# A new order for the front of a convolution and quantised matmul kernel, with the conv in two parts

## The chip, the core and the metric

The kernel runs on one core of a Trainium2 chip. The metric is the time of one execution on the device, in microseconds (us).

Five engines work side by side, each through its own list of instructions in order: TensorE (PE, with its weight loads as PEld), VectorE (DVE), ScalarE (ACT), GpSimd (POOL) and SyncE (SP), which here only issues transfers. An instruction can wait for a semaphore that another engine raises; everything behind it on its own engine then waits too.

## The reference, cut to what matters

```python
# x: (64, 64, 1024)   conv in 4 groups of 16 channels, 9 taps, pad 4
out = conv(x, weight) + (cond @ c_weight.T)[:, :, None] + cond_bias[None, :, None]
def fake_quant(v, bits, axis):          # integer levels times a scale
    bound = 2 ** (bits - 1) - 1
    scale = max(abs(v), axis) / bound
    return round(clip(v / scale, -bound, bound)) * scale
xq = fake_quant(out, 8, axis=-1)        # one scale per row of 1024
kq = fake_quant(kernel, 8, axis=0)      # (1024, 1024), one scale per output column
y = xq @ kq + fake_quant(bias, 16, axis=-1)
result = x + fake_quant(y, 8, axis=-1)
```

## The kernel before

The 4096 rows of 1024 are cut into 32 tiles of 128 rows (`TILES`): 8 samples times the 16 channels of one conv group. In all loops `t` is a tile and `k` a step; the work of one tile is spread over six or more steps.

For one tile, in the order in which the data flows:

- `load_xwin(t)` (SP, L170) brings the windows of x. `round_x(t)` (ACT, L287) makes the rounded part `x_hi`; `split(t)` (POOL, L229) makes the rest `x_lo` from both.
- `conv(t)` (PE, L404) is 2 matmuls for the condition term (`select` against `ctx2`), then three groups of 4: `x_hi` with `w_hi`, `x_hi` with `w_lo`, `x_lo` with `w_hi`. Only the last group needs `x_lo`. The result takes 2 of the PSUM banks `conv_ps`, which two tiles use in turn.
- `column_max(t)` (DVE, L602) takes the largest magnitudes, `spread_max(t)` (PE, L429) brings them across partitions, `levels(t)` (DVE, L619) makes the inverse scale and the integer levels of samples 0 to 3, and `round_levels(t)` (ACT, L325) those of samples 4 to 7.
- `turn_levels(t)` (PE, L437) transposes the levels into `turn_ps`, `take_levels(t)` (ACT, L317) copies them to `a_t`.
- `dense(t, h)` (PE, L447) is 8 matmuls for half `h` of the 1024 output columns. `scale_half(t, h)` (DVE, L583) applies the scales; `add_bias` adds the quantised bias, on DVE for half 0 and on POOL for half 1.
- `out_scale(t)` (DVE, L649), `quantise(t)` (ACT, L335: two activations of 1024) and `add_x(t)` (POOL, L245) finish the tile, and SP stores it. `outs(k)` says which tiles do so in step `k`. It is one tile in a step, except in steps 15 and 20, where it is two, since the second halves of `dense` catch up by one step at tiles 10 and 16 (`CATCH_UP`).

Beside this stands the front, done once. The 1024 x 1024 matrix is loaded as 8 blocks in 4 pairs, 1 MB each (`load_k`). `k_levels(pair)` (DVE, L555) waits for a pair, takes its maxima, makes scale and inverse, and rounds those of its two blocks that are in `DVE_K`; `k_round(fb)` (ACT, L294) rounds the others (`ACT_K`). `k_turn(user)` (PE, L461) transposes a block into a PSUM bank of `dense_ps` and `k_take(user)` (ACT, L299) copies it to `kq`; two of the ten users are the scales themselves. Since `dense_ps` is also where `dense` writes, the users from 5 on have one bank, and each waits for the take of the one ahead. `bias_scale` (DVE) and `bias_levels` (ACT) quantise the bias, which a transfer of 512 KB spreads over all partitions. The condition term is two small matmuls on PE, then three DVE instructions (L542 to L547) that end in `ctx_made`, for which `conv(0)` waits. `warm_up` (L389) is 2 matmuls of ident by ident, twice.

The whole order of work is written out by hand in one list per engine (DVE from L683, ACT from L352, PE from L492, POOL from L252, SP from L174). The front lies in steps 0 to 4: `k_levels(k + 1)` stands behind `column_max(k)` on DVE, and the users of the bank lie between the convs and the dense halves on PE.

Of the kernel before, what the change touches and what calls it, by code (L numbers as in the profile page):

```python
# [32 lines left out]
ACT_K = (1, 3)  # L33
DVE_K = (0, 2, 4, 5, 6, 7)
# [4 lines left out]
def build(nc, xw, xr, wt, cond_t, cw_t, cond_bias, ker, bias, out):  # L39
    with ExitStack() as ctx:  # L40
# [6 lines left out]
        def sem(name):  # L47
# [27 lines left out]
        b_row = sb("b_row", [P, F], F32)  # L75
# [27 lines left out]
        turn_ps = ps("turn_ps", [P, NS, P], I16)  # L103

# [5 lines left out]
            "k_turned", "k_taken", "b_max_made", "b_scale_made", "b_inv_made",  # L110
# [44 lines left out]
        def k_bank(user):  # L155
            return dense_ps[:, user % 2 if user < 5 else 1, :]

        K_USERS = (0, 1, 2, 3, "scale0", 4, 5, 6, 7, "scale1")
# [5 lines left out]
        def _(sp):  # L164
# [51 lines left out]
        def _(pool):  # L216
# [50 lines left out]
        def _(act):  # L267
            act.dma_start(condt[:], cond_t).then_inc(s["cond_in"], 16)
# [40 lines left out]
            def bias_levels():  # L309
                act.wait_ge(s["b_inv_made"], 1)  # L310
                act.activation(b_int[:], b_row[:], ACT.Copy, scale=b_stat[:, 2:3]
# [45 lines left out]
            for k in range(second_step(LAST) + 2):  # L357
                if k == 2:
                    take_levels(1)
                    k_take(5)  # L360
                    k_take(6)
                    round_x(4)
                    bias_levels()
                elif k == 3:
                    k_take(7)
                    k_take(8)
                    take_levels(2)
                    round_x(5)
                else:
                    if k == 4:  # L370
                        k_take(9)
                    if there(k - 1):
                        take_levels(k - 1)
                    if there(k + 2):
                        round_x(k + 2)
                if k == 0:
                    k_round(3)
                    k_take(2)
                    k_take(3)
                    k_take(4)  # L380
                for t in outs(k):
                    quantise(t)
                if there(k):
                    round_levels(k)
            quantise_last()

        @block.tensor
        def _(pe):
            def warm_up():  # L389
                for i in range(WARM):  # L390
                    pe.matmul(dense_ps[:, 1, :].rearrange("p (i f) -> p i f", f=P), ident[:],
# [4 lines left out]
            warm_up()  # L396
            pe.wait_ge(s["cond_made"], 1)
# [6 lines left out]
            def conv(t):  # L404
                at, g, n0 = t % 2, t % GROUPS, t // GROUPS * NS
                x_at = t % XSPLIT
                wait(pe, "a_rounded_dve", t - 1)
                wait(pe, "a_rounded", t - 1)
                wait(pe, "hi_made", t + 1)
                for hs in range(2):  # L410
                    ns = slice(n0 + hs * NH, n0 + (hs + 1) * NH)
                    mm = pe.matmul(  # L412
                        conv_ps[:, at, hs, :].rearrange("p (n b) -> p n b", n=NH),
                        ctx2[:, g].rearrange("k q o -> k (q o)"),
                        select[:, ns].unsqueeze(2).to_broadcast([P, NH, BLOCKS]),
                        start=True, stop=False, skip_group_check=True)
                for x, w in ((x_hi, w_hi), (x_hi, w_lo), (x_lo, w_hi)):
                    if x is x_lo:
                        wait(pe, "lo_made", t + 1)
                    for ch in range(2):  # L420
# [6 lines left out]
                mm.then_inc(s["conv_made"], 1)  # L427
# [9 lines left out]
            def turn_levels(t):  # L437
                wait(pe, "a_rounded_dve", t + 1)
                wait(pe, "a_rounded", t + 1)
                wait(pe, "a_made", t)  # L440
                for j in range(NS):
# [5 lines left out]
            def dense(t, h):  # L447
# [5 lines left out]
                if t == 0:  # L453
                    pe.wait_ge(s["k_taken"], k_taken_of(f"scale{h}"))
# [6 lines left out]
            def k_turn(user):  # L461
                wait(pe, "k_taken", user if user > 5 else user - 1)
# [21 lines left out]
            pe.wait_ge(s["w_lo_made"], 2)  # L484
# [7 lines left out]
            for k in range(TILES):  # L492
                again = seconds(k)
                if k == 4:
                    k_turn(9)
                conv(k)
                if k == 0:
                    k_turns(0, 1)
                if k == 1:
                    k_turns(2, 4)  # L500
                if k == 3:
                    k_turns(7, 8)
                if k in (2, 3):
                    dense(k - LAG, 0)
                    turn_levels(k - 1)
                    if k == 2:
                        k_turns(5, 6)
                    spread_max(k)
                elif k == 1:
                    spread_max(k)  # L510
                    turn_levels(k - 1)
                else:
                    if there(k - 1):
                        turn_levels(k - 1)
                    if len(again) == 2:
                        dense(again[0], 1)
                    if there(k - LAG):
                        dense(k - LAG, 0)
                    spread_max(k)
                    if again:  # L520
                        dense(again[-1], 1)
# [7 lines left out]
        def _(dve):  # L529
# [10 lines left out]
                            ).then_inc(s["same_b_made"], 1)  # L540
            dve.wait_ge(s["ctx_mm"], 1)
# [12 lines left out]

            def k_levels(pair):  # L555
                fs = slice(2 * pair, 2 * pair + 2)
                dve.wait_ge(k_in[pair], 16)
                dve.tensor_reduce(k_max[:, fs], k_raw[:, fs, :], AX_X, ALU.max,  # L558
                                  apply_absolute_value=True).then_inc(s["k_max_made"], 1)
                dve.wait_ge(s["k_max_made"], pair + 1)  # L560
                dve.tensor_scalar(k_scale[:, fs], k_max[:, fs], 1.0 / 127, TINY, ALU.mult,
                                  ALU.max).then_inc(s["k_scale_made"], 1)
                dve.wait_ge(s["k_scale_made"], pair + 1)
                dve.reciprocal(k_inv[:, fs], k_scale[:, fs]).then_inc(s["k_inv_made"], 1)
                dve.wait_ge(s["k_inv_made"], pair + 1)
# [183 lines left out]
```

## Time and profile before

| | us |
|---|---|
| median of 3 runs | 283.77 (283.61 to 284.38) |
| the profiled execution | 282.26 |
| its span from first to last instruction | 280.5 |
| PE busy | 253.2 (90%) |
| DVE busy | 211.9 (76%) |
| POOL busy | 194.2 (69%) |
| ACT busy | 185.0 (66%) |

The profile shows one execution. It has a page of totals, and its trace answers questions: the timeline lists instructions of an engine in order of time with start, duration and the idle time ahead of them; the windows view gives the busy time of each engine in a stretch; the waits name who waited for whom. Busy times of PE are modelled from pipelined matmuls: the duration of a group of matmuls reaches to the end of the last one, some 0.15 us past the time at which the next group can start.

### The profile page before, as it was taken

What the parts mean: (1) busy time and instruction counts of PE and PEld (TensorE: products, weight loads), DVE (VectorE), ACT (ScalarE), POOL (GpSimd) and SP (SyncE); (2) the same over time, 40 slices, a digit from 0 to 9 for tenths busy, and PEclk for the clock granted to TensorE, in tenths of its full rate; (3) what the DMA queues carried; (4) which work ended last, traced back from release to release, by engine and by line L of the source; (5) the groups of instructions that cost most, each with busy time, mean ns of one, the idle gap of its engine ahead of it and who ended that gap; (6) DMA issues with size and microseconds to landing.
All of it is one profiled execution on the core that took longest, in us unless ns stands there. A gap on an engine that the chain in (4) does not pass through costs nothing.

```text
span 280.5 us, 4237 instructions
## 1 busy us (share of the span) xinstructions
PE 253.2 (90%) x1372; PEld 165.0 (59%) x1372; DVE 211.9 (76%) x447; ACT 185.0 (66%) x278; POOL 194.2 (69%) x104
## 2 busy tenths in 40 slices
PE   7966869999999999999899999799999999999800
PEld 3555557666666666666566566566666666665300
DVE  2598974668777778777978677967778888777674
ACT  4257686446777767667986567867777777755662
POOL 3533332544888888879897788997888888845973
PEclk9979999999999999999999999999999999999975
DMA  6999323530566665646677645565666664444424
GB/s 230 407 411 355 103 92 141 167 137 0 196 220 199 222 211 201 195 167 198 226 272 256 188 155 198 211 239 213 227 225 225 221 232 152 150 151 152 151 116 183
DMA packets 15800, 56.05 MB, mean 200 GB/s; under 512 B 1954, under 2 KB 1954, under 8 KB 15778
## 3 DMA queue, kind: packets, MB, share of 16 engines
q1 hardware_dynamic: 15488, 55.71, 56.2%
q8 instruction: 11, 0.18, 0.3%
q10 hardware_dynamic: 290, 0.07, 0.1%
q14 instruction: 11, 0.09, 0.1%
HBM read 38.99 MB, written 16.78 MB: 199 GB/s over the span
## 4 chain that ended last, share of the span: by engine, by line
POOL 49%; issue 41%; DVE 3%; DMA 3%; ACT 1%; SPq 0%; POOLq 0%; DVEq 0%; PE 0%
POOL x_lo L233 26%; POOL y L241 15%; POOL o_sb L249 8%; DMA k_raw<-ffn_kernel 3%; DVE k_max L558 1%; ACT kq L305 1%; DVE o_sb L665 1%; DVE y_max L656 0%; ACT x_hi L291 0%; SPq L175 0%; DVE k_int L569 0%; DVE dense_ps L590 0%; ACT y_int L349 0%; DVE y L599 0%; DVE last_max L673 0%
## 5 line engine op out<-in xcount | busy, mean ns | idle before, releaser
L456 PE MATMUL dense_ps<-kq,a_t 128*128 128x512 bf16 x496 | 116.7, 379 | 0.0
L233 POOL TENSOR_TENSOR x_lo<-xwin,x_hi 128x1032 fp32r<-128x1032 f32 x32 | 76.6, 2393 | 51.6 <-ACT x_hi L291 51.6
L249 POOL TENSOR_TENSOR o_sb<-y,o_sb 128x1024 f32<-128x1024 f32 x31 | 73.9, 2386 | 24.6 <-ACT y L341 24.6
L456 PEld LDWEIGHTS dense_ps<-kq,a_t 128*128 128x128 bf16 x496 | 47.6, 101 | 45.1 <-issue 0.3
L604 DVE TENSOR_REDUCE small_ps<-conv_ps 128x8 f32<-128x1024 f32 x32 | 39.4, 1232 | 39.6 <-PE conv_ps L422 39.5
L321 ACT CAST a_t<-turn_ps 128x1024 bf16<-128x1024 int16 x32 | 32.4, 1012 | 48.7 <-PE turn_ps L442 48.7
L338 ACT ACTIVATE y_int<-y,y_inv 128x1024 int16<-128x1024 f32 x31 | 35.6, 1147 | 24.1 <-DVE y_inv L647 24.1
L241 POOL TENSOR_TENSOR y<-y,bq 128x512 f32<-128x512 f32 x33 | 41.8, 1273 | 1.0 <-DVE y L590 1.0
L656 DVE TENSOR_REDUCE y_max<-y 128x1 f32<-128x1024 f32 x31 | 37.5, 1211 | 2.3 <-POOL y L241 2.0
L330 ACT ACTIVATE a_int<-conv_ps,inv 128x128 int16<-128x128 f32 x128 | 36.1, 363 | 1.9 <-DVE inv L625 1.9
L291 ACT CAST x_hi<-xwin 128x1032 fp32r<-128x1032 f32 x32 | 33.8, 1055 | 5.3 <-DMA xwin<-x_windows 5.3
L341 ACT ACTIVATE y<-y_int,y_scale 128x1024 f32<-128x1024 int16 x31 | 35.7, 1151 | 1.0
L422 PE MATMUL conv_ps<-x_hi,w_hi 128*128 128x512 f32 x128 | 36.3, 406 | 0.0
L422 PE MATMUL conv_ps<-x_hi,w_lo 128*128 128x512 f32 x128 | 35.8, 401 | 0.0
L422 PE MATMUL conv_ps<-x_lo,w_hi 128*128 128x512 f32 x128 | 35.2, 397 | 0.0
L422 PEld LDWEIGHTS conv_ps<-x_hi,w_lo 128*128 128x128 f32 x128 | 24.5, 192 | 6.2
L422 PEld LDWEIGHTS conv_ps<-x_hi,w_hi 128*128 128x128 f32 x128 | 25.0, 196 | 5.0
L422 PEld LDWEIGHTS conv_ps<-x_lo,w_hi 128*128 128x128 f32 x128 | 24.1, 188 | 6.1
L412 PE MATMUL conv_ps<-select,ctx 128*128 128x512 f32 x64 | 26.0, 489 | 1.6 <-ACT x_hi L291 1.6
L590 DVE SCALAR_TENSOR_TENSOR dense_ps<-dense_ps,row_scale,k_scale_b 128x512 f32<-128x512 f32 x31 | 23.1, 744 | 4.9 <-PE dense_ps L456 4.9
L442 PE MATMUL turn_ps<-ident_b,a_int 128*128 128x128 bf16 x256 | 19.8, 220 | 5.2 <-issue 3.5
L590 DVE SCALAR_TENSOR_TENSOR y<-dense_ps,row_scale,k_scale_b 128x512 f32<-128x512 f32 x31 | 23.0, 743 | 1.4 <-PE dense_ps L456 1.4
(62 smaller groups left out, 209.1 us busy)
## 6 DMA issues: line engine op xcount, KB each, us to landing
xwin<-x_windows SPq DMA_DIRECT2D x32, 516.0 KB, 4.7
o_sb<-x_rows SPq DMA_DIRECT2D x32, 512.0 KB, 4.5
out<-o_sb SPq DMA_DIRECT2D x31, 512.0 KB, 2.9
k_raw<-ffn_kernel SPq DMA_DIRECT2D x4, 1024.0 KB, 11.9
w_raw<-taps SPq DMA_DIRECT2D x2, 256.0 KB, 3.0
b_row<-ffn_bias SPq DMA_DIRECT2D x1, 512.0 KB, 15.1
out<-o_sb SPq DMA_DIRECT2D x2, 256.0 KB, 2.7
condt<-cond_t ACTq DMA_DIRECT2D x1, 32.0 KB
```

Source lines behind the costliest of these rows:

```text
L233: pool.tensor_tensor(x_lo[:, at].rearrange("p n b -> p (n b)"), xwin[:, t % XWIN, :], x_hi[:, at].bitcast(F32).rearrange("p n b -> p (n b) ...
L241: pool.tensor_tensor(y[:, t % YRING, half(h)], y[:, t % YRING, half(h)], bq[:, half(h)], ALU.add).then_inc(s["biased1" if h else "biased0_ ...
L249: pool.tensor_tensor(o_sb[:, at, :], y[:, t % YRING, :], o_sb[:, at, :], ALU.add).then_inc(s["o_made"], 1)
L291: act.copy(x_hi[:, t % XSPLIT].rearrange("p n b -> p (n b)"), xwin[:, t % XWIN, :]).then_inc(s["hi_made"], 1)
L330: ins = act.activation(a_int[:, at, n * BLOCKS:(n + 1) * BLOCKS], conv_cols(at)[:, n, :], ACT.Copy, scale=inv8[:, at, n:n + 1])
L338: act.activation(y_int[:, t % 2], y[:, t % YRING, :], ACT.Copy, scale=y_inv[:, t % 2:t % 2 + 1]).then_inc(s["y_rounded"], 1)
L341: act.activation(y[:, t % YRING, :], y_int[:, t % 2], ACT.Copy, scale=y_scale[:, t % 2:t % 2 + 1]).then_inc(s["y_dequantised"], 1)
L422: mm = pe.matmul(conv_ps[:, at, hs, :].rearrange("p (n b) -> p n b", n=NH), w[:, ch, g].rearrange("p q o -> p (q o)"), x[:, x_at, hs * NH: ...
L456: mm = pe.matmul(dense_bank(t, h), a_t[:, t % LEVELS, q].rearrange("b j o -> b (j o)"), kq[:, q, half(h)], start=(q == 0), stop=(q == Q - 1))
L590: dve.scalar_tensor_tensor(out=to, in0=dense_bank(t, h), scalar=row_scale[:, t % RSRING:t % RSRING + 1], in1=k_scale_b[:, half(h)], op0=AL ...
L604: dve.tensor_reduce(cmax_ps, conv_ps[:, t % 2].rearrange("p h (n b) -> p (h n) b", b=BLOCKS), AX_X, ALU.max, apply_absolute_value=True).th ...
L656: dve.tensor_reduce(y_max[:, at], y[:, t % YRING, :], AX_X, ALU.max, apply_absolute_value=True).then_inc(s["y_max_made"], 1)
```

## The change

- Transfers: on SP's queue the first pair of kernel blocks goes ahead of the conv weights and x; the last pair goes behind the windows of tile 2. The bias is no longer spread by a 512 KB transfer: 4 KB come into one partition, as the first transfer on ACT's queue, and two matmuls of `ones` spread it over the partitions into `dense_ps`.
- DVE: `bias_scale` and `k_levels(0)` come first, ahead of the three instructions of the condition term. In `k_levels` the scale of a pair is made by two instructions of one column each, in place of one of two columns. `k_levels(1)` comes ahead of `column_max(0)`, `k_levels(2)` behind `column_max(2)` and `scale_half(0, 0)`, `k_levels(3)` behind `column_max(3)` and `scale_half(1, 0)`. For tiles 0 and 1 DVE makes the levels of all 8 samples (`WHOLE`).
- The blocks that ACT rounds are 0, 1, 5, 7 in place of 1, 3; DVE rounds the other four.
- PE: `conv` can be called in two parts, `conv_start` (condition term and `x_hi` with `w_hi`) and `conv_rest`. Steps 0 to 4 are written out anew with spreads, turns and users of the bank between the parts. The first scale goes through `turn_ps`. The warm-up matmuls write there too.
- POOL: `split(1)`, `split(3)` and `split(4)` wait until DVE has rounded 2, 3 and 4 blocks.
- ACT: the order in front follows. From step 5 on, where two tiles are quantised in a step, `round_levels` comes between them and no longer behind both.

```diff
-ACT_K = (1, 3)
-DVE_K = (0, 2, 4, 5, 6, 7)
+ACT_K = (0, 1, 5, 7)
+DVE_K = (2, 3, 4, 6)
+WHOLE = 2
...
-        K_USERS = (0, 1, 2, 3, "scale0", 4, 5, 6, 7, "scale1")
+            if user == 2:
+                return turn_f32
+            return dense_ps[:, 0 if user in (0, 3) else 1, :]
+
+        K_USERS = (0, 1, "scale0", 2, 3, 4, 5, 6, 7, "scale1")
...
+            load_k(0)
             for ch in range(2):
                 sp.dma_start(w_raw[:, ch].rearrange("p q g o -> p (q g o)"), wt[ch]
                              ).then_inc(w_in[ch], 16)
             load_xwin(0)
-            load_k(0)
             load_k(1)
             load_xwin(1)
             load_k(2)
+            load_xwin(2)
             load_k(3)
-            load_xwin(2)
-            sp.dma_start(b_row[:], bias.partition_broadcast(P)).then_inc(s["b_in"], 16)
             load_xwin(3)
...
             def split(t):
                 wait(pool, "hi_made", t + 1)
+                wait(pool, "k_rounded_dve", {1: 2, 3: 3, 4: 4}.get(t, 0))
...
+            act.dma_start(b_row[:], bias.unsqueeze(0)).then_inc(s["b_in"], 16)
             act.dma_start(condt[:], cond_t).then_inc(s["cond_in"], 16)
...
             round_x(0)
+            bias_levels()
+            k_round(0)
             k_round(1)
-            k_take(0)
-            k_take(1)
             round_x(1)
...
+            for user in range(5):
+                k_take(user)
+            round_x(2)
+            take_levels(0)
+            round_x(3)
+            take_levels(1)
+            round_x(4)
+            k_round(5)
+            k_take(5)
+            round_levels(2)
+            take_levels(2)
+            k_take(6)
+            round_x(5)
+            k_round(7)
+            round_levels(3)
+            k_take(7)
+            k_take(8)
+            take_levels(3)
+            k_take(9)
+            round_x(6)
+            round_levels(4)
+            for k in range(5, second_step(LAST) + 2):
+                if there(k - 1):
+                    take_levels(k - 1)
+                if there(k + 2):
+                    round_x(k + 2)
+                for t in outs(k)[:1]:
                     quantise(t)
                 if there(k):
                     round_levels(k)
+                for t in outs(k)[1:]:
+                    quantise(t)
...
             warm_up()
+            pe.wait_ge(s["b_in"], 16)
+            for h in range(2):
+                pe.matmul(dense_ps[:, h, :], ones[0:1, :], b_row[:, half(h)], start=True, stop=True
+                          ).then_inc(s["b_spread"], 1)
             pe.wait_ge(s["cond_made"], 1)
...
             def k_turn(user):
-                wait(pe, "k_taken", user if user > 5 else user - 1)
+                wait(pe, "k_taken", user if user >= 5 else (0, 0, 0, 1, 2)[user])
...
+            conv(0)
+            k_turns(0, 2)
+            conv_start(1)
+            k_turns(3, 4)
+            spread_max(0)
+            conv_rest(1)
+            turn_levels(0)
+            conv_start(2)
+            spread_max(1)
+            conv_rest(2)
+            turn_levels(1)
+            dense(0, 0)
+            conv_start(3)
+            spread_max(2)
+            conv_rest(3)
+            k_turn(5)
+            turn_levels(2)
+            dense(1, 0)
+            k_turn(6)
+            conv_start(4)
+            spread_max(3)
+            conv_rest(4)
+            k_turns(7, 8)
+            turn_levels(3)
+            k_turn(9)
+            dense(2, 0)
+            spread_max(4)
+            dense(0, 1)
+            for k in range(5, TILES):
...
+            bias_scale()
+            k_levels(0)
             dve.wait_ge(s["ctx_mm"], 1)
...
-            k_levels(0)
-            for k in range(TILES):
+            k_levels(1)
+            column_max(0)
+            levels(0)
+            column_max(1)
+            levels(1)
+            column_max(2)
+            scale_half(0, 0)
+            k_levels(2)
+            levels(2)
+            add_bias(0, 0)
+            column_max(3)
+            scale_half(1, 0)
+            k_levels(3)
+            levels(3)
+            add_bias(1, 0)
+            for k in range(4, TILES):
```

## Rows read from the trace of the kernel before

**Rows 1.** The page's span, and its busy times by engine (first line of them).

```profile
span 280.5 us, 4237 instructions
PE 253.2 (90%) x1372; PEld 165.0 (59%) x1372; DVE 211.9 (76%) x447; ACT 185.0 (66%) x278; POOL 194.2 (69%) x104
```

**Rows 2.** Windows: length; busy PE, PEld, DVE, ACT, POOL (instructions); PE clock; DMA; GB/s.

```profile
10.00:20.00 10.00, 7.51 (x37) 5.67 (x37) 9.20 (x8) 4.03 (x4) 3.82 (x2) 0.89 1.03 415
40.00:50.00 10.00, 7.79 (x59) 5.88 (x58) 4.92 (x11) 6.74 (x14) 2.98 (x2) 1.00 0.29 106
50.00:60.00 10.00, 10.00 (x55) 6.26 (x54) 6.45 (x14) 5.07 (x8) 4.27 (x3) 1.00 0.61 213
```

**Rows 3.** Timeline (start, duration, engine, line, count): first matmuls of conv(4), conv(5), conv(6).

```profile
46.01 0.68 PE L412 MATMUL conv_ps<-select,ctx 128*128 128x512 f32 x2
...
53.26 0.78 PE L412 MATMUL conv_ps<-select,ctx 128*128 128x512 f32 x2
...
60.59 0.78 PE L412 MATMUL conv_ps<-select,ctx 128*128 128x512 f32 x2
```

**Rows 4.** Timeline: the first 16 us on PE and DVE, and the bias maximum.

```profile
1.43 3.78 PE L391 MATMUL dense_ps<-ident 128*128 128x512 f32 x4 [1.43 <-POOL ident L219]
...
6.30 0.22 DVE L542 CAST ctx_r<-small_ps 128x64 fp32r<-128x64 f32 x1 [4.07 <-PE small_ps L400]
...
7.08 0.69 DVE L547 TENSOR_TENSOR ctx<-small_ps,ctx_r 64x512 fp32r<-64x512 f32 x1
...
9.25 1.58 PE L412 MATMUL conv_ps<-select,ctx 128*128 128x512 f32 x2
...
10.60 2.29 DVE L558 TENSOR_REDUCE k_max<-k_raw 128x2 f32<-128x2048 f32 x1 [2.83 <-DMA k_raw<-ffn_kernel]
...
29.41 1.21 DVE L575 TENSOR_REDUCE b_stat<-b_row 128x1 f32<-128x1024 f32 x1
```

**Rows 5.** DMA issues in the first 24 us: size, median us to landing.

```profile
k_raw<-ffn_kernel SPq DMA_DIRECT2D x4, 1024.0 KB, 11.9
```

**Rows 6.** Timeline: POOL's split beside DVE's scale instructions, at 17.7 and at 66.8.

```profile
17.74 2.38 POOL L233 TENSOR_TENSOR x_lo<-xwin,x_hi 128x1032 fp32r<-128x1032 f32 x1 [6.18 <-ACT x_hi L291]
17.82 2.32 DVE L561 TENSOR_SCALAR k_scale<-k_max 128x2 f32<-128x2 f32 x1
...
66.75 2.38 POOL L233 TENSOR_TENSOR x_lo<-xwin,x_hi 128x1032 fp32r<-128x1032 f32 x1 [3.18 <-ACT x_hi L291]
66.90 0.15 DVE L644 TENSOR_SCALAR y_scale<-y_max 128x1 f32<-128x1 f32 x1
```

**Rows 7.** Timeline: the first turn, and the pieces of one round of the front.

```profile
27.34 0.61 PE L442 MATMUL turn_ps<-ident_b,a_int 128*128 128x128 bf16 x8 [1.64 <-ACT a_int L330]
...
31.08 1.90 PE L456 MATMUL dense_ps<-kq,a_t 128*128 128x512 bf16 x8
...
32.69 2.27 DVE L558 TENSOR_REDUCE k_max<-k_raw 128x2 f32<-128x2048 f32 x1
...
35.40 1.42 DVE L569 TENSOR_SCALAR k_int<-k_raw,k_inv 128x1024 int16<-128x1024 f32 x2
...
36.73 0.75 DVE L590 SCALAR_TENSOR_TENSOR dense_ps<-dense_ps,row_scale,k_scale_b 128x512 f32<-128x512 f32 x1
...
38.15 2.41 POOL L233 TENSOR_TENSOR x_lo<-xwin,x_hi 128x1032 fp32r<-128x1032 f32 x1 [5.74 <-ACT x_hi L291]
38.51 1.10 PE L422 MATMUL conv_ps<-x_lo,w_hi 128*128 128x512 f32 x4
...
41.21 1.03 ACT L305 CAST kq<-dense_ps 128x1024 bf16<-128x1024 int16 x1
```

**Rows 8.** Timeline: four conv matmuls just after PE had stood idle.

```profile
18.73 1.91 PE L422 MATMUL conv_ps<-x_hi,w_hi 128*128 128x512 f32 x4
```

**Rows 9.** Timeline at step 15: ACT's levels, and the turn behind them.

```profile
139.56 1.12 ACT L330 ACTIVATE a_int<-conv_ps,inv 128x128 int16<-128x128 f32 x4
...
140.79 0.61 PE L442 MATMUL turn_ps<-ident_b,a_int 128*128 128x128 bf16 x8 [1.41 <-issue]
```

More of the change, by code:

```diff
@@ L74, in build @@
         kq = sb("kq", [P, Q, F], BF16)
-        b_row = sb("b_row", [P, F], F32)
+        b_row = sb("b_row", [1, F], F32)
         b_stat = sb("b_stat", [P, 4], F32)
@@ L310, in bias_levels @@
                 act.wait_ge(s["b_inv_made"], 1)
-                act.activation(b_int[:], b_row[:], ACT.Copy, scale=b_stat[:, 2:3]
+                act.activation(b_int[:], bias_ps, ACT.Copy, scale=b_stat[:, 2:3]
                                ).then_inc(s["b_rounded"], 1)
@@ L402, in _, with terms @@
             warm_up()
[L404 to L417, printed above, removed]
+            def terms(t, pairs):
+                at, g, x_at = t % 2, t % GROUPS, t % XSPLIT
+                for x, w in pairs:
                     if x is x_lo:
                         wait(pe, "lo_made", t + 1)
+                    if t == 0 and w is w_lo:
+                        pe.wait_ge(s["w_lo_made"], 2)
                     for ch in range(2):
@@ L426, in conv, with conv_start, conv_rest @@
                                 start=False, stop=False, skip_group_check=True)
-                mm.then_inc(s["conv_made"], 1)
+                return mm
+            def conv_start(t):
+                at, g, n0 = t % 2, t % GROUPS, t // GROUPS * NS
+                wait(pe, "a_rounded_dve", t - 1)
+                wait(pe, "a_rounded", t - 1 - WHOLE)
+                wait(pe, "hi_made", t + 1)
+                for hs in range(2):
+                    ns = slice(n0 + hs * NH, n0 + (hs + 1) * NH)
+                    pe.matmul(
+                        conv_ps[:, at, hs, :].rearrange("p (n b) -> p n b", n=NH),
+                        ctx2[:, g].rearrange("k q o -> k (q o)"),
+                        select[:, ns].unsqueeze(2).to_broadcast([P, NH, BLOCKS]),
+                        start=True, stop=False, skip_group_check=True)
+                terms(t, ((x_hi, w_hi),))
+            def conv_rest(t):
+                terms(t, ((x_hi, w_lo), (x_lo, w_hi))).then_inc(s["conv_made"], 1)
+            def conv(t):
+                conv_start(t)
+                conv_rest(t)
             def spread_max(t):
@@ L453, in dense @@
                 if t == 0:
-                    pe.wait_ge(s["k_taken"], k_taken_of(f"scale{h}"))
+                    pe.wait_ge(s["k_taken"], len(K_USERS) * (h + 1) // 2)
                 for q in range(Q):
@@ L490, in k_turns @@
                     k_turn(user)
-            for k in range(TILES):
+            conv(0)
[27 more added lines that the diff above has]
+            for k in range(5, TILES):
                 again = seconds(k)
-                if k == 4:
-                    k_turn(9)
                 conv(k)
[L497 to L521, printed above, removed]
+                turn_levels(k - 1)
+                if len(again) == 2:
+                    dense(again[0], 1)
+                dense(k - LAG, 0)
+                spread_max(k)
+                dense(again[-1], 1)
             dense(LAST - 1, 0)
@@ L681, in out_scale_last @@
                 scale_of(LAST)
-            k_levels(0)
-            for k in range(TILES):
+            k_levels(1)
[14 more added lines that the diff above has]
+            for k in range(4, TILES):
                 again = seconds(k)
                 column_max(k)
-                if k < 3:
-                    k_levels(1 + k)
                 if len(again) == 2:
@@ L692, in _ @@
                     out_scale(t)
-                if there(k - LAG):
-                    scale_half(k - LAG, 0)
+                scale_half(k - LAG, 0)
                 levels(k)
-                if k == 1:
-                    bias_scale()
-                if there(k - LAG) and not pool_adds(k - LAG, 0):
+                if not pool_adds(k - LAG, 0):
                     add_bias(k - LAG, 0)
-                if again:
-                    scale_half(again[-1], 1)
+                scale_half(again[-1], 1)
             out_scale(LAST - 3)
```

103 lines of the change are left out of this document (42 added, 61 removed).

## The prediction

> **What bounds the kernel now.** I read the windows first. From 50 us on PE is busy in all of a stretch, while between 10 and 50 us it has gaps [rows 2]. Then the timeline of PE: conv(5) starts at 53.26 and conv(6) at 60.59, so a step lasts 7.33 us, and the step from conv(4) at 46.01 already lasts 7.25 [rows 3]. PE is 90% busy over the span of 280.5 us [rows 1], and its gaps lie in three places: the front, a pause at each of the two steps with two quantised tiles, and the tail behind its last matmul. So the change is worth what it does to the start of conv(5), behind which the old and new loops give PE the same list, plus what it does to the two pauses. The tail's lists are untouched.
>
> In the front the bound is a chain through several engines. DVE is busy 9.2 of 10 us between 10 and 20, on kernel blocks and maxima [rows 2]. The first turn waits until 27.34 for ACT's half of the levels [rows 7], and DVE's scale of the second pair took 2.32 us beside POOL's split where such an instruction takes 0.15 beside another split [rows 6].
>
> **How I cost it.** I lay out the instructions of the four engines in their new order, each starting when its engine is free and what it waits for is done, with the durations of the rows. The old order laid out in the same way puts conv(5) at 53.7, where the trace has 53.26. The layouts are compared with each other, so that this offset of 0.4 drops out.
>
> **The start: conv(0) comes 5.2 us later.** PE's warm-up of four passes takes 3.78 us from 1.43, some 0.85 a pass [rows 4]. The two matmuls that spread the bias have the same 512 columns in f32, so four passes more: 3.4 us, and the bias is spread at about 8.4. `bias_scale` stands first on DVE: 1.21 us for the maximum [rows 4] and 0.4 for two small instructions, to 10.05. `k_levels(0)` follows: 2.29 for the maxima [rows 4], three small ones at 0.15 to 0.17 with gaps, to 12.95. Queued behind are the three instructions of the condition term, which took 6.30 to 7.77 before [rows 4] and now end at 14.4. conv(0) waits for them and starts at 14.4 in place of 9.25 [rows 4]. Everything else is ready: x_hi at 11.7, w_lo at 12.0.
>
> Transfers: before, 1 MB of the first pair, issued third, landed at 10.6 by the idle time that its landing ended [rows 4], with a median of 11.9 for a pair [rows 5]. Put first it should land near 8, and the weights and the first x 2.5 to 5 us later than now (near 9 and 10.6). None of these is the last thing waited for, since DVE reaches the first pair at 10.05. With all landings 2 us later the layout moves by 0.3 only. So the new place of the first pair gains nothing here, the dropped 512 KB gain nothing, and the new SP order costs nothing. The extra issue on ACT's queue puts ACT about 0.5 us back, under PE's bias matmuls.
>
> **Steps 0 to 2: a lead of 5.4 us.** `k_levels(1)` runs from 14.4 to 18.8 with both its blocks rounded. Its scale is now made by instructions of one column, and the one-column instruction took 0.15 us beside a split [rows 6], so the 2.32 is gone. DVE makes all levels of tiles 0 and 1 (1.33 in place of 0.69 each) and the first turn no longer waits for ACT. It comes at 24.2, not 27.34 [rows 7], conv(2) at 24.9 and conv(3) at 30.7, where the old layout has 27.7 and 36.1.
>
> **Steps 3 and 4: the lead is lost, and 6.0 us more.** Here the change adds waits. `split(3)` waits for the third block that DVE rounds, which is in `k_levels(2)`. That stands on DVE behind `scale_half(0, 0)`, which waits for `dense(0, 0)`. The chain in the layout: dense(0, 0) done at 30.9, scale 0.75, maxima 2.27, small ones 0.6, first rounding 0.75, done at 35.4; the split 2.41, done at 37.8; only then the last third of conv(3), 1.10 [rows 7]. PE has nothing else to do in its list and stands from 33.3 to 37.8: 4.5 us. Behind conv_rest(3) stand turn of block 4, ACT's take 1.03 [rows 7], ACT's levels 1.12 [rows 9] since `round_levels(2)` is queued behind that take, turn_levels(2) and dense(1, 0), 1.90 [rows 7]. That is done at 44.0, and the ring closes: `scale_half(1, 0)`, `k_levels(3)`, fourth rounding at 48.5, split(4) to 50.9, conv_rest(4) to 51.9, a second stall of 4.1 us. Then two blocks and a scale go through one bank in turn with takes of 1.03 and 0.6 between them, then dense(2, 0) and dense(0, 1). One round of this ring is 0.75 + 2.27 + 0.6 + 0.75 + 2.41 + 1.1 + 0.6 + 1.03 + 1.12 + 0.6 + 1.9 = 13.1 us, against 7 to 10 us for a step in the old front. conv(4) comes at 44.2 (old layout 46.3) and conv(5) at 59.7 (old 53.7). **Front: +6.0.**
>
> The rows explain why somebody would want these waits: the 2.32 beside the split [rows 6] is DVE's instruction held until POOL's ended. The Trainium skill (SBUF — State Buffer, "Who interferes with whom") says that tensor_scalar in a two-port mode and GpSimd exclude each other for a whole instruction. By it the waits save at most one hold of a rounding for each. The trace agrees with the hold; the price of a hold, 2.3, is less than the 4.5 and 4.1 that the layout shows for the waits.
>
> **The two pauses: -2.4.** At step 15 the turn starts at 140.79 behind ACT's levels, which end at 139.56 + 1.12, and PE stood 1.6 us there (conv(16) at 135.77 plus 3.43 is 139.2) [rows 9]. With `round_levels` between the quantised tiles the levels end at 138.8, in time. But the second quantise then pushes the take and the next round_x, and the layout shows waits of 0.27 and 0.20 in the next step. So 1.1 to 1.6 are saved at each of the two steps, 2.2 to 3.1 together; I take 2.4, nearer to the lower end because ACT is late by one activation of 1.15.
>
> **Clock: +1.5.** Before, the four matmuls that followed PE's idle time at 16 to 17.7 took 1.91 in place of 1.10 [rows 7, 8], and the granted clock between 10 and 20 was 0.89 on the mean [rows 2]. That is a spell at the lower level (1.2 GHz). The new layout has three idle times of PE that are longer: 2.4 us ahead of conv(0), 4.5 and 4.1 at the splits. A spell behind the first costs 1.3 in the layout, behind the other two 1.5 to 1.9 together; the old spell is already in the old layout. Bounds 0 and +2.8. I take half.
>
> **Unknowns of the start.** If the clock rises before the bias matmuls, they take half: -1.4. The reciprocal of two columns now runs beside `split(0)`, which the trace does not show; between no hold and a hold like the 2.32 from which the split's head start goes off, 0 to +1.4. I take 0 for both.
>
> **Sum.** 6.0 - 2.4 + 1.5 = +5.1 us. On the profiled execution: 282.26 + 5.1 = 287.4. The median of the runs is 1.5 above that execution, so I put the sum on it: 283.77 + 5.1 = 288.9. Low end of this case: 6.0 - 3.1 + 0 - 1.4 = +1.5 (285.3); high end: 6.0 - 1.9 + 2.8 + 1.4 = +8.3 (292.1).
>
> **Rivals.**
> - The lead is kept (faster). If the third and fourth roundings were done before PE needs the splits, the ring would not close on the waits. Laid out with the two splits free, conv(5) comes at 53.9 and the end 2.7 us earlier than before: 281.1. It decides at split(3): it would have to start by 30.9, and the rounding ends at 35.4 in my layout. DVE would have to be 4.5 us ahead, and the two items of the start, which I took at 0, give at most 1.4. For it: conv(3) is 5.4 ahead, and what I call a stall rests on the order of DVE's list. Chance 0.11.
> - Both things small (no change). The early clock (-1.4), full pauses gained (-3.1), no slow spells, and a ring some 1.5 shorter than I add up, for instance if takes overlap with the turns: 6.0 - 1.4 - 3.1 - 1.5 = 0, 283.8. Chance 0.08.
> - The pauses are not gained. If the second quantise holds the next levels as long as it held the first ones, the term of -2.4 is 0: 291.3 with the clock as taken. Against it: a step has 7.33 us and ACT's instructions fill some 5.5 of them. Chance 0.08.
> - That the front doesn't matter at all, since something behind it makes up for a late conv(5), is excluded by PE's full stretches [rows 2].
>
> **How the numbers follow.** My case, with its bounds, has the rest: 0.73. The range of 284.0 to 292.0 holds this case, the third rival and part of the second, and leaves the faster one out. This kernel can be told from no change at about 0.3%, 0.85 us. Slower: 0.73 + 0.08 and a part of the second, 0.82; within: 0.07; faster: 0.11.
>
> **What would show it.** In the new profile: the first matmul of conv(0) near 14.4, conv(3) near 30.7, conv(5) near 59.7 or later; PE idle for 4 us and more ahead of the `x_lo` matmuls of conv(3) and conv(4), put down to POOL's x_lo; POOL idle ahead of these splits until DVE's k_int; clock rows below 1.00 between 10 and 60 us; no pause ahead of the turns at steps 15 and 20. I am wrong if conv(5) comes before 56, or if PE does not wait for x_lo at conv(3).

## The result and the profile after

The changed kernel takes 290.68 us (288.24 to 292.05), against 283.81 us for the kernel before: 1.025 times as long, 95% interval 1.018 to 1.033. Beside a later group of experiments it took 290.95 against 283.15, 1.029 (1.024 to 1.033). The forecast was 288.9 us, range 284.0 to 292.0. One execution each of c1_pairs_first and c3_ctx_first lay more than 1.5% above the fastest of its kernel; the ratios leave it out.

The profiled execution took 291.26 us. First the page of the changed kernel: its span, its busy times, and the granted clock in 40 slices of 7.2 us (tenths of full speed).

```profile
span 289.4 us, 4243 instructions
...
PE 260.0 (90%) x1376; PEld 168.3 (58%) x1376; DVE 211.2 (73%) x449; ACT 185.2 (64%) x272; POOL 193.6 (67%) x104
...
PEclk9579977869999999999999999999999999999995
```

The work is the same, 4243 instructions against 4237. The span grew by 8.9 us [rows 1]. The clock line has low tenths in its first nine slices; after that PE is at its full clock until the tail.

The windows of the changed kernel (length; busy PE, PEld, DVE, ACT, POOL; clock; DMA share; GB/s) show where the time went.

```profile
10.00:20.00 10.00, 8.38 (x30) 5.09 (x29) 8.44 (x14) 4.99 (x6) 4.63 (x3) 0.60 1.02 410
20.00:30.00 10.00, 10.00 (x75) 8.02 (x73) 5.85 (x15) 7.25 (x8) 3.21 (x2) 1.00 0.43 144
30.00:40.00 10.00, 5.77 (x31) 3.95 (x30) 7.21 (x14) 3.11 (x3) 2.36 (x1) 0.92 0.26 100
40.00:50.00 10.00, 7.81 (x44) 5.04 (x42) 3.94 (x4) 4.71 (x8) 0.00 (x0) 0.74 0.29 104
50.00:60.00 10.00, 5.57 (x36) 4.12 (x36) 4.72 (x13) 5.28 (x9) 4.70 (x2) 0.78 0.48 172
```

Between 20 and 30 us PE now has work all the time, more than before. Then come 30 us in which no engine is full: PE 5.8, 7.8 and 5.6 of 10, DVE 7.2, 3.9 and 4.7, and POOL does nothing at all between 40 and 50. Before, the stretch from 50 to 60 was already full on PE [rows 2]. Half-idle engines everywhere are the mark of a chain that goes around through all of them. And PE's busy time there is partly slow time, since the clock is 0.74 and 0.78.

The timeline of the changed kernel: the first matmuls of conv(0), conv(3), conv(4) and conv(5), and the two stalls between them, with a block's turn and a dense half behind the first.

```profile
14.31 1.19 PE L441 MATMUL conv_ps<-select,ctx 128*128 128x512 f32 x2 [1.62 <-DVE ctx L614]
...
31.85 0.78 PE L441 MATMUL conv_ps<-select,ctx 128*128 128x512 f32 x2
...
38.97 2.07 PE L427 MATMUL conv_ps<-x_lo,w_hi 128*128 128x512 f32 x4 [4.23 <-POOL x_lo L238]
40.84 1.08 PE L508 MATMUL dense_ps<-ident_b,k_int 128*128 128x128 bf16 x8
...
44.56 2.92 PE L484 MATMUL dense_ps<-kq,a_t 128*128 128x512 bf16 x8
...
48.09 0.97 PE L441 MATMUL conv_ps<-select,ctx 128*128 128x512 f32 x2
...
54.24 1.22 PE L427 MATMUL conv_ps<-x_lo,w_hi 128*128 128x512 f32 x4 [3.08 <-POOL x_lo L238]
...
65.24 0.78 PE L441 MATMUL conv_ps<-select,ctx 128*128 128x512 f32 x2
```

What the splits waited for stands on DVE and POOL: `scale_half(0, 0)`, the third rounding and split(3), then `scale_half(1, 0)`, the fourth rounding and split(4), whose row also holds split(5).

```profile
32.24 0.76 DVE L629 SCALAR_TENSOR_TENSOR dense_ps<-dense_ps,row_scale,k_scale_b 128x512 f32<-128x512 f32 x1 [0.75 <-PE dense_ps L484]
...
35.66 0.75 DVE L592 TENSOR_SCALAR k_int<-k_raw,k_inv 128x1024 int16<-128x1024 f32 x1
...
36.55 2.36 POOL L238 TENSOR_TENSOR x_lo<-xwin,x_hi 128x1032 fp32r<-128x1032 f32 x1 [7.96 <-DVE k_int L592]
...
47.51 0.76 DVE L629 SCALAR_TENSOR_TENSOR dense_ps<-dense_ps,row_scale,k_scale_b 128x512 f32<-128x512 f32 x1 [4.94 <-PE dense_ps L484]
...
50.94 0.75 DVE L592 TENSOR_SCALAR k_int<-k_raw,k_inv 128x1024 int16<-128x1024 f32 x1
...
51.83 4.70 POOL L238 TENSOR_TENSOR x_lo<-xwin,x_hi 128x1032 fp32r<-128x1032 f32 x2 [12.91 <-issue]
```

The dense half releases the scale, the scale's queue holds the rounding, the rounding releases the split, and PE stands until the split is done. That is the ring, gone round twice.

conv(5) starts at 65.24 where it started at 53.26 [rows 3], 12.0 us later. The span is 8.9 us longer. So 3.1 us came back behind conv(5), at the two pauses. Here is the new timeline of the first of them: conv and turn on PE, ACT's levels between the two quantised tiles.

```profile
147.76 0.78 PE L441 MATMUL conv_ps<-select,ctx 128*128 128x512 f32 x2
...
149.65 1.14 ACT L336 ACTIVATE a_int<-conv_ps,inv 128x128 int16<-128x128 f32 x4 [0.22 <-DVE inv L664]
150.67 1.17 ACT L344 ACTIVATE y_int<-y,y_inv 128x1024 int16<-128x1024 f32 x1
...
151.21 0.62 PE L470 MATMUL turn_ps<-ident_b,a_int 128*128 128x128 bf16 x8
```

The levels are done at 150.8, the turn starts at 151.21, 3.45 us behind the conv's start, with no idle time of PE ahead of it. Before, that turn stood 1.4 us and more [rows 9].

### The profile page after: what moved, and what is told of

Same layout as the page of the kernel before. It is cut to its first block, busy times and chain, and to the rows that moved or that the text cites. A ratio compares the mean times of both kernels' runs of the same rounds, so it can differ in the third digit from the quotient of the medians.

```text
span 289.4 us, 4243 instructions
## 1 busy us (share of the span) xinstructions
PE 260.0 (90%) x1376; PEld 168.3 (58%) x1376; DVE 211.2 (73%) x449; ACT 185.2 (64%) x272; POOL 193.6 (67%) x104
## 4 chain that ended last, share of the span: by engine, by line
POOL 43%; issue 39%; DVE 2%; POOLq 0%; ACT 0%; DVEq 0%
POOL x_lo L238 20%; POOL y L246 14%; POOL o_sb L254 9%; DVE o_sb L705 1%; DVE y_max L696 0%; DVE dense_ps L629 0%; ACT y_int L355 0%; DVE y L638 0%; DVE last_max L713 0%; DVEq L41 0%; POOLq L132 0%; POOLq L253 0%; DVE y_scale L684 0%; DVE y_inv L687 0%; DVE y_max L719 0%
## 5 line engine op out<-in xcount | busy, mean ns | idle before, releaser
L484 PE MATMUL dense_ps<-kq,a_t 128*128 128x512 bf16 x496 | 118.2, 383 | 0.0
L427 PE MATMUL conv_ps<-x_lo,w_hi 128*128 128x512 f32 x128 | 36.3, 406 | 7.3 <-POOL x_lo L238 7.3
L336 ACT ACTIVATE a_int<-conv_ps,inv 128x128 int16<-128x128 f32 x120 | 33.8, 363 | 3.2 <-DVE inv L664 3.2
L629 DVE SCALAR_TENSOR_TENSOR dense_ps<-dense_ps,row_scale,k_scale_b 128x512 f32<-128x512 f32 x31 | 23.0, 742 | 13.1 <-PE dense_ps L484 13.1
L441 PE MATMUL conv_ps<-select,ctx 128*128 128x512 f32 x64 | 25.4, 480 | 1.6 <-DVE ctx L614 1.6
L673 DVE TENSOR_TENSOR a_int<-conv_ps,inv 128x512 int16<-128x512 f32 (+1 forms) x32 | 23.2, 725 | 0.0
```

What stands on the lines that cost most here:

```text
L336: ins = act.activation(a_int[:, at, n * BLOCKS:(n + 1) * BLOCKS], conv_cols(at)[:, n, :], ACT.Copy, scale=inv8[:, at, n:n + 1])
L427: mm = pe.matmul(conv_ps[:, at, hs, :].rearrange("p (n b) -> p n b", n=NH), w[:, ch, g].rearrange("p q o -> p (q o)"), x[:, x_at, hs * NH: ...
L484: mm = pe.matmul(dense_bank(t, h), a_t[:, t % LEVELS, q].rearrange("b j o -> b (j o)"), kq[:, q, half(h)], start=(q == 0), stop=(q == Q - 1))
L629: dve.scalar_tensor_tensor(out=to, in0=dense_bank(t, h), scalar=row_scale[:, t % RSRING:t % RSRING + 1], in1=k_scale_b[:, half(h)], op0=AL ...
```

## The experiments

Theory 1 is the ring of waits of the prediction. Theory 2 is that low spells of TensorE's clock, which follow the stalls, add to it. The main rival is the late start of conv(0). Ratios are against the kernel before beside the same group. The changed kernel was measured twice, at 1.0251 and 1.0285 of the kernel before; the gains below are counted from the second, and would be 1.0 us smaller from the first.

**Splits free (a1_splits_free).** The changed kernel, the waits of split(3) and split(4) taken out.

```diff
-                wait(pool, "k_rounded_dve", {1: 2, 3: 3, 4: 4}.get(t, 0))
+                wait(pool, "k_rounded_dve", {1: 2}.get(t, 0))
```

> The changed kernel, with split(3) and split(4) no longer waiting for DVE's third and fourth rounding (split(1) still waits). Theory 1, the ring of waits: PE no longer stands ahead of the x_lo matmuls of conv(3) and conv(4) (4.2 and 3.1 us in the changed kernel), a rounding beside a split may be held up to 2.3 us, conv(5) starts near 56 to 58 in place of 65.2, and the median is 282 to 285. Rival, the start: the loss comes from conv(0) starting 5 us late; then the stalls only move to other waits and the median stays at 288 or above.

Measured: 284.59 us, ratio 1.0054 (1.0016 to 1.0092), against 1.0285 for the changed kernel: 6.5 us less. Both stalls ahead of x_lo are gone, conv(5) starts at 56.66. conv(0) is as late as ever, at 14.89. The rival is out: a late conv(0) alone doesn't keep the median at 288. What the waits were to prevent does happen once, here in the timeline of this kernel (POOL's split, DVE's rounding of a block):

```profile
43.12 2.38 POOL L238 TENSOR_TENSOR x_lo<-xwin,x_hi 128x1032 fp32r<-128x1032 f32 x1 [9.26 <-ACT x_hi L297]
...
44.06 2.00 DVE L592 TENSOR_SCALAR k_int<-k_raw,k_inv 128x1024 int16<-128x1024 f32 x1
```

The rounding takes 2.00 in place of 0.75. So the two waits save 1.25 us of DVE here and cost 6.5 us of the whole.

**Pairs first (c1_pairs_first).** All waits kept, the order of DVE's list changed.

```diff
-            scale_half(0, 0)
             k_levels(2)
+            scale_half(0, 0)
             levels(2)
...
-            scale_half(1, 0)
             k_levels(3)
+            scale_half(1, 0)
             levels(3)
```

> The changed kernel with all its waits, but with k_levels(2) ahead of scale_half(0, 0) and k_levels(3) ahead of scale_half(1, 0) on DVE. Theory 1 says that the loss is a ring: dense half, scale, pair of blocks, split, conv, turn, take, levels, dense half. With the pair ahead of the scale the ring is open though the waits are all there: laid out with the durations of the trace, conv(5) comes 5.3 us earlier, and with fewer slow clock spells the median falls to 283 to 286. Rival, the waits themselves: POOL still waits for the third and fourth rounding, so PE stands as long, 289 to 291.

Measured: 282.41 us, ratio 0.9991 (0.9955 to 1.0028): 8.3 us less than the changed kernel, with every wait in place, and more than I expected (283 to 286): conv(5) came at 56.43, 8.8 us earlier, where the layout had 5.3. This is the sharpest of the tests. The waits were harmful because of what stood ahead of the roundings on DVE: `scale_half`, which waits for PE's dense half, which waited for the conv. With the pair ahead of it, this is what PE waited for between 8 and 60 us:

```profile
PE conv_ps L427 <- POOL x_lo L238: 2.7, 1, 2.7
PE turn_ps L470 <- issue: 2.2, 1, 2.2
PE conv_ps L441 <- DVE ctx L614: 1.3, 1, 1.3
PE dense_ps L508 <- ACT kq L311: 1.1, 1, 1.1
PE dense_ps L499 <- ACT kq L311: 0.7, 1, 0.7
```

One stall at x_lo is left, 2.7 us; the second is gone. The first line of the same view of the changed kernel (us in total, times, longest):

```profile
PE conv_ps L427 <- POOL x_lo L238: 7.3, 2, 4.2
```

**Both (c2_pairs_first_free).**

> The same order as c1_pairs_first, and split(3) and split(4) don't wait for the roundings. Laid out: another 2.9 us earlier than c1, the end 3 us earlier than with the waits dropped alone, so 279 to 282 if no rounding is held by a split, 281 to 284 if one or two are held by up to 2.3 us each.

Measured: 279.34 us, ratio 0.9879 (0.9831 to 0.9928). 3.1 us less than c1, as laid out. Against the waits dropped alone (a1) it is 5.0 us by the ratios, where I had 3. No x_lo wait of PE is left.

**Filled stalls (a3_fill).** All as in the changed kernel, but PE multiplies into a free bank while it would stand idle (FILL is 16).

```diff
+                    if x is x_lo and t in (3, 4):
+                        wait(pe, "a_made", t - 1)
+                        for _ in range(FILL):
+                            pe.matmul(turn_f32, ident_b[:], kq[:, 0, 0:HALF], start=True, stop=True)
                     if x is x_lo:
                         wait(pe, "lo_made", t + 1)
```

> The changed kernel with 16 matmuls of 512 columns (some 3.5 us at the full clock, results unused) put into turn_ps ahead of the x_lo matmuls of conv(3) and conv(4), where PE stands idle anyway. Theory 2, the clock: the spells at the lower level that follow these two idle times (38.4 to 41.9 and 55.5 to 62.3 in the changed kernel) go, and the median falls by 2 to 4 us, to 287 to 289. Rival, the ring alone: the stalls have the same ends, the fill changes nothing or costs up to 1 us, 290 to 292.

Measured: 286.25 us, ratio 1.0106 (1.0049 to 1.0164): 5.1 us less than the changed kernel by the ratios, though 32 useless matmuls were added and no wait was removed. The timeline of PE in this kernel, the fill and what follows:

```profile
35.33 3.63 PE L425 MATMUL turn_ps<-kq,ident_b 128*128 128x512 bf16 x16
39.72 1.22 PE L432 MATMUL conv_ps<-x_lo,w_hi 128*128 128x512 f32 x4 [0.76 <-POOL x_lo L239]
40.77 0.62 PE L513 MATMUL dense_ps<-ident_b,k_int 128*128 128x128 bf16 x8
...
54.29 1.21 PE L432 MATMUL conv_ps<-x_lo,w_hi 128*128 128x512 f32 x4 [0.26 <-POOL x_lo L239]
...
63.22 0.78 PE L446 MATMUL conv_ps<-select,ctx 128*128 128x512 f32 x2
```

The four matmuls take 1.22 where the changed kernel's took 2.07, and the block's turn behind them 0.62 where it took 1.08. From the x_lo matmuls of conv(4) to conv(5) it is 8.93 us, where the changed kernel took 11.00. Theory 2 holds, and the effect is larger than the 2 to 4 us that I expected: 5.1 us (4.1 from the first measurement of the changed kernel), beside 7.3 us of the stalls themselves. The profiled execution is the longest of the six, 289.18, and still had low spells (9.3 to 19.6 and 43.5 to 46.9), none from 46.9 to the tail; the other five took 285.7 to 287.4.

**Condition term first (a4_ctx_first).** `bias_scale()` and `k_levels(0)` back behind the three instructions of the condition term on DVE.

> The changed kernel with DVE's three instructions of the condition term back ahead of bias_scale and k_levels(0). conv(0) should start near 11.5 in place of 14.3. If the late start matters (rival), the median falls by 2 us or more. By theory 1 DVE's list bounds the front from 14 us on and the ring after it, so most of it is absorbed: the median falls by 0 to 1.5 us.

Measured: 290.71 us, ratio 1.0247 (1.0181 to 1.0313), against 1.0285 (1.0237 to 1.0333): no difference that can be told. The profile shows the shortest of the four executions, 288.74 us; the others took 290.7 to 290.8. In it conv(0) started at 11.51, 2.8 us earlier than in the changed kernel's profile, and conv(5) at 62.81, still 2.4 us earlier, though the two stalls were longer together (4.24 and 3.73 us). So in this one execution most of the lead was kept, and in the median it doesn't show.

**The same with the ring open (c3_ctx_first).** That edit on top of c2.

> The kernel c2_pairs_first_free with DVE's three instructions of the condition term ahead of bias_scale and k_levels(0) as well. With the ring open, does the late start of conv(0) count? Laid out, conv(0) comes 2.5 us earlier and conv(5) 0.1 earlier, since DVE's pairs bound the steps between: the same as c2 within 0.7 us, 278.7 to 280. If the late start is a cost of its own, 277 to 278.

Measured: 278.19 us, ratio 0.9843 (0.9791 to 0.9895), c2 having 0.9879 (0.9831 to 0.9928). That lies between what I had for "the same" (278.7 to 280) and for a cost of its own (277 to 278), and the two intervals lie over each other. The one profiled execution is 282.33 us, far from the median, with conv(0) at 13.91, so no trace shows how early conv(0) comes in the others. a4 and c3 each give 1.0 to 1.1 us in the ratio, within the noise; a late start worth 2 us isn't excluded.

**split(0) later (a5_split0_later).**

```diff
                 wait(pool, "hi_made", t + 1)
+                wait(pool, "ctx_made", 0 if t else 2)
```

> The changed kernel with one more wait: split(0) waits for ctx_made, so that POOL no longer runs beside DVE's copy of the condition term (which took 2.02 us there against 0.49 before). If that is a hold, the copy takes 0.5, conv(0) starts near 12.8 in place of 14.3, and 0 to 1.5 us of it reach the end. Rival: the copy is slow for another reason and stays at 2.0.

Measured: 291.26 us, ratio 1.029 (1.0234 to 1.0345), no gain, and conv(0) at 14.89 in its profile, not at 12.8. The copy took 0.42, as expected of a hold, but the execution was not the one that I had costed: in it the bias matmuls took 3.78 us and not 1.98, DVE came to the copy 2.2 us later, and then the split would not have been beside it anyway. So this run did not tell the two apart. The changed kernel itself did, in two executions with and without overlap. First the one above, then the one of after_again (split of tile 0 on POOL, copy on DVE):

```profile
10.67 2.38 POOL L238 TENSOR_TENSOR x_lo<-xwin,x_hi 128x1032 fp32r<-128x1032 f32 x1
...
11.31 2.02 DVE L611 CAST ctx<-ctx_r 64x512 fp32r<-64x512 f32 x1
```

```profile
10.65 2.37 POOL L238 TENSOR_TENSOR x_lo<-xwin,x_hi 128x1032 fp32r<-128x1032 f32 x1
...
13.49 0.42 DVE L611 CAST ctx<-ctx_r 64x512 fp32r<-64x512 f32 x1
```

Beside the split the copy ends 0.28 us after the split does (13.33 and 13.05); behind it, it takes 0.42. It is held.

**The changed kernel again (after_again).**

> The changed kernel as it is, beside the others: 2.5% over the kernel before, 290 to 291. If the spread of its times comes from the clock, the executions with the higher mean granted clock are the shorter ones.

Measured: 290.95 us (289.88 to 292.66), ratio 1.0285 (1.0237 to 1.0333). As expected, the shorter executions are here those with the higher clock: ordered by their time, from 289.88 to 292.66, they had mean clocks of 0.963, 0.960, 0.956, 0.944, 0.944 and 0.938. It isn't a strict rule: of the first four executions of this kernel one took 292.05 us at 0.963 and one 291.26 at 0.944. The kernel before varies in the same way: with clocks of 0.975 and up it took 280.7 to 282.3, with 0.968 and less 283.2 to 284.6.

**New pauses alone (b1_new_pause).** The kernel before, with one edit.

```diff
-                for t in outs(k):
+                for t in outs(k)[:1]:
                     quantise(t)
                 if there(k):
                     round_levels(k)
+                for t in outs(k)[1:]:
+                    quantise(t)
```

> The kernel before, with only the new order of ACT where two tiles are quantised in one step (round_levels between them). The pauses of PE ahead of the turns at steps 15 and 20, 1.6 us each, go: 280.7 (3.1 less) if nothing else gives way, 281.6 (2.2 less) if the second quantise delays the next step as I laid out. Rival: no gain, 283.8.

Measured: 280.09 us, ratio 0.9889 (0.9833 to 0.9944), 3.1 us less. This part of the change is a plain gain by itself, and it hid a part of the loss.

**New pauses and all levels on DVE (b2_pause_whole).** On top of b1, `WHOLE = 2`: DVE makes the levels of all samples of tiles 0 and 1.

```diff
-                half_n = NS // 2
+                mine = NS if t < WHOLE else NS // 2
...
-                if there(k):
+                if there(k) and k >= WHOLE:
                     round_levels(k)
...
-                wait(pe, "a_rounded", t + 1)
+                wait(pe, "a_rounded", t + 1 - WHOLE)
```

> The kernel before with the new order at the two pauses and with WHOLE = 2 (DVE makes all levels of tiles 0 and 1, so that the first turn doesn't wait for ACT), nothing else of the change. Laid out, 1.6 us less than with the pauses alone: 278 to 279, level with c2. Rival: DVE, the busiest engine there, is late instead, 280 or more.

Measured: 277.47 us, ratio 0.9816 (0.9779 to 0.9854). Beside the next experiment it took 277.50, ratio 0.9788 (0.9739 to 0.9838); the expectation for that one was:

> The kernel b2_pause_whole as it is, on the same chip as b3_one_column: 277.2 to 277.8, 2% under the kernel before.

The first turn starts at 25.52 and no longer waits for ACT, where it waited until 27.34 [rows 7]. By the ratios that is 2.1 us less than with the pauses alone, a little more than the 1.6 laid out. With two small edits this kernel is 5.2 to 6.0 us under the kernel before by the ratios, the largest gain here but for b3, which is level with it.

**One-column scales on top (b3_one_column).**

```diff
-                dve.tensor_scalar(k_scale[:, fs], k_max[:, fs], 1.0 / 127, TINY, ALU.mult,
-                                  ALU.max).then_inc(s["k_scale_made"], 1)
+                for fb in (2 * pair, 2 * pair + 1):
+                    dve.tensor_scalar(k_scale[:, fb:fb + 1], k_max[:, fb:fb + 1], 1.0 / 127, TINY,
+                                      ALU.mult, ALU.max).then_inc(s["k_scale_made"], 1)
...
```

> The kernel b2_pause_whole with the scale of a pair made by two instructions of one column each, as in the changed kernel. If the small scale instruction was the one that the split held (2.32 us), it is free now; but the rounding of 1024 behind it would start at 17.1 while the split runs to 18.9, and would be held in its place. I expect 0 to 0.4 us less, 277.1 to 277.6. Rival, as my prediction had it (the 2.32 is gone): up to 2 us less on DVE.

Measured: 277.35 us, ratio 0.9794 (0.9745 to 0.9844), the same as without it. The timelines tell why. First b2_again, then b3_one_column, POOL's split(1) and DVE beside it:

```profile
17.19 2.38 POOL L234 TENSOR_TENSOR x_lo<-xwin,x_hi 128x1032 fp32r<-128x1032 f32 x1 [6.25 <-ACT x_hi L292]
17.49 2.10 DVE L564 TENSOR_SCALAR k_scale<-k_max 128x2 f32<-128x2 f32 x1
19.62 0.17 DVE L567 RECIPROCAL k_inv<-k_scale 128x2 f32<-128x2 f32 x1
19.82 0.75 DVE L572 TENSOR_SCALAR k_int<-k_raw,k_inv 128x1024 int16<-128x1024 f32 x1
```

```profile
17.23 2.38 POOL L234 TENSOR_TENSOR x_lo<-xwin,x_hi 128x1032 fp32r<-128x1032 f32 x1 [6.26 <-ACT x_hi L292]
17.39 0.21 DVE L565 TENSOR_SCALAR k_scale<-k_max 128x1 f32<-128x1 f32 x2
17.64 0.17 DVE L568 RECIPROCAL k_inv<-k_scale 128x2 f32<-128x2 f32 x1
17.84 2.32 DVE L573 TENSOR_SCALAR k_int<-k_raw,k_inv 128x1024 int16<-128x1024 f32 x1
```

The one-column instructions pass, the rounding behind them is held in their place. The scale's row ends with the split (19.59 and 19.57), the rounding's 0.55 us behind it (20.16 and 19.61). On DVE the rounding is done 0.4 us earlier than without the edit, and the time doesn't show it.

## Why the prediction was right, and what in it was not

- **What bounds: right.** PE's steady steps are untouched (7.34 us, conv(5) to conv(6)), so the change was worth what it did to conv(5) and to the pauses.
- **The start, conv(0) at 14.4: right in the sum, by luck in the terms.** It came at 14.31. In that execution the bias matmuls took 1.98 us and not 3.4, which was my low bound of -1.4, and the copy was held, 2.02 us and not 0.49, which I had not thought of; I had bounded a hold of the reciprocal, which passed beside a split in 0.17 (b3). In after_again the same matmuls took 3.77, the copy 0.42, and conv(0) came at 14.89. The 3.4 was too low for that case: 0.85 a pass is less than the row's 3.78 us over four passes, some 0.94.
- **The late start costs little: right in the main.** a4 and c3 show 1.0 to 1.1 us by the ratios, within the noise, and a1 that the loss goes with conv(0) as late as ever. How much of the 2.8 us is kept to the end isn't settled: one execution of a4 kept 2.4 to conv(5).
- **Transfers cost nothing: nearly right.** In the changed kernel ACT waited 2.31 us for the last small transfer of the condition term, which landed at 7.3, and PE then stood 0.95 us ahead of its two matmuls for the condition term. DVE came to the result only at 11.05, so that this wait was covered. No pair of blocks was waited for.
- **The lead at conv(3): right.** I had 30.7 in place of 36.10, a lead of 5.4. In after_again conv(3) came at 30.77. In the first profile it came at 31.85, behind a low spell of the clock from 7.9 to 18 us in which two groups of four matmuls of conv(0) took 1.91 and 1.53 us in place of 1.10 each.
- **The 2.32 us of DVE's scale: gone, but not by the one-column instructions.** b3 shows that these alone hand the hold on to the rounding. In the changed kernel split(1) waits for both roundings, which end at 18.27, and starts at 18.42, so that nothing was beside it.
- **The ring: right**, mechanism, place and order. Stalls of 4.23 and 3.08 us at x_lo of conv(3) and conv(4), for which I had 4.5 and 4.1. From the end of one stall to the end of the next it was 15.3 us, where one round had 13.1; conv(5) came at 65.24, not at 59.7. The difference is in the clock, below. Theory 1 was tested from two sides: without the waits (a1) and with the waits but another order (c1), 6.5 and 8.3 us less.
- **The pauses: mis-sized.** I took -2.4, they gave -3.1 (b1), the upper bound. The step that failed is the pair of small waits that I laid into the following step: between 60 and 240 us PE of b1 has no wait at all. The high end of my sum took -1.9 for this term, below my own lower bound of 2.2; with 2.2 it is +8.0, 291.8 us, and the range stands.
- **The clock: the term that was too small.** I took +1.5 of a bound of 2.8. With the front at +6.0 and the pauses at -3.1, the measured +6.9 to +7.8 leave 4.0 to 4.9 for it, and filling two stalls gave back 5.1 (a3). The rows agree. Behind the first stall the x_lo matmuls, a block's turn and the dense half took 2.07, 1.08 and 2.92 us, in place of 1.10, 0.62 and 1.89: 2.5 us. From the x_lo matmuls of conv(4) to conv(5) it was 11.00 us, in place of the 8.93 of a3, whose clock was full there: 2.1 more. I had priced only the matmuls that directly follow each stall. In the changed kernel the clock was low, beside the spell at the start, from 38.4 to 41.9, 45.3 to 48.7 and 55.5 to 62.3, and since every part of the ring waits for PE once in a round, slow transposes, scale turns and dense halves all lay on the chain: 2.07 us for a scale turn in place of 1.11.
- **The rival "the lead is kept"** gave 281.1 with the splits free. Made true in a1 it came to 284.6, its profiled execution to 282.6 with conv(5) at 56.66 and not 53.9. In that one a rounding was held for 1.25 us more and the clock was low from 47.0 to 53.9, neither of which was in that layout.
- **The rule of the Trainium skill** (SBUF — State Buffer, "Who interferes with whom") weighed in the prediction, that such instructions of DVE and GpSimd exclude each other: the runs agree, 2.00, 2.02, 2.10 and 2.32 us for instructions that take 0.17 to 0.75. By it the waits looked worth having; the price on the chain, 6.5 us, decided against them.

What stays open: how much of the new front beside the ring is worth something. With the ring open (c2, 0.9879) the whole new order equals the old one with only the new pauses (b1, 0.9889); the new places of the transfers, the bias and the first pair were not run one by one, and the wait of split(1) stood in every kernel with the new front.

## What to carry to other kernels

A wait that keeps two instructions apart costs nothing as long as what it waits for doesn't itself wait for the result: before adding one, follow the awaited instruction back through its engine's list, for everything ahead of it there is part of the wait. When all engines are half idle at once, look for such a ring, and mend it by the order of one list before taking waits away. A stall of TensorE in a chain can cost more than its own length: here the clock fell behind two stalls of 7.3 us together, and matmuls put into them gave back 5.1.

## What the runs showed of the hardware that I had not expected

- Useless matmuls in a stall were worth 5.1 us. In the changed kernel PE had no work between 34.7 and 38.9, and the spell at the lower level began at 38.4, so the work that ended the stall was already slow: 2.07 us for four matmuls that take 1.10 [rows 7].
- Two executions of the same program took different ways in the first 10 us. The four passes of the bias matmuls took 1.98 us in one and 3.77 in the other, a factor of 1.9. The granted clock reads 1.00 in both stretches, so that the rows don't show the cause. Then the two parted again: behind 0.95 us of idle time the granted clock of the first was at 0.50 from 7.9 to 18 us, that of the second stayed at 1.00 to 38 us. Here both are, PE's timeline of the changed kernel's profile and of after_again:

```profile
4.75 1.98 PE L409 MATMUL dense_ps<-b_row,ones 1*128 1x512 f32 x4
```

```profile
5.13 3.77 PE L409 MATMUL dense_ps<-b_row,ones 1*128 1x512 f32 x4
```

- A copy of 64 x 512 is held by a split (2.02 us in place of 0.42), while a one-column scale (0.15 beside a split [rows 6], 0.21 for two in b3) and a reciprocal of two columns (0.17 in b3) are not.
